# The mixtures' second product with tokens in the rows, its sums added from PSUM, and the second bias spread and added by GpSimd

## The reference, cut to what is computed

```python
x = L0_attn_a_x                                   # (2, 2048, 256), float32
x = x + _L0_attn_a_ref(_layernorm(x))             # 16 heads, causal
x = x + _L0_ffn_ref(_layernorm(x), Wr, W1, b1, W2, b2)
x = x + _L0_attn_b_ref(_layernorm(x), Wq, ...)    # distance attention
x = x + _L0_ffn_ref(_layernorm(x), Wr, W1, b1, W2, b2)

def _L0_ffn_ref(x, Wr, W1, b1, W2, b2):           # "mixture": 2 of 8 experts for each batch
    logits = x.mean(axis=1) @ Wr
    top_scores, top_idx = jax.lax.top_k(logits, 2)
    weights = jax.nn.softmax(top_scores, axis=-1)
    h = einsum('btd,bkdf->bktf', x, W1[top_idx]) + b1[top_idx][:, :, None, :]   # f = 1024
    h = gelu(h)
    y = einsum('bktf,bkfd->bktd', h, W2[top_idx]) + b2[top_idx][:, :, None, :]
    return einsum('bk,bktd->btd', weights, y)
```

## Time and profile before

| | |
|---|---|
| device time, median of three (lowest to highest) | 1783.35 us (1781.84 to 1784.34) |
| device time of the profiled execution | 1783.04 us |
| its span from first to last instruction | 1781.3 us |
| TensorE matmul busy | 1706.9 us, 96% |
| TensorE weight load busy | 1171.9 us, 66% |
| VectorE busy | 1062.4 us, 60% |
| ScalarE busy | 953.9 us, 54% |
| GpSimd busy | 352.7 us, 20% |
| mean granted TensorE clock | 0.993 |

### The profile page before, as it was taken

How to read it: one execution, slowest core, us unless ns; L and a number is a source line. 1 busy time by engine, 2 the same in 40 slices (tenths; PEclk the granted TensorE clock), 3 DMA queues, 4 the chain that set the end, 5 groups by cost and what they waited for, 6 DMA issues and landing times. The chain is left out here.

```text
span 1781.3 us, 28593 instructions
## 1 busy us (share of the span) xinstructions
PE 1706.9 (96%) x10767; PEld 1171.9 (66%) x10767; DVE 1062.4 (60%) x2216; ACT 953.9 (54%) x1258; POOL 352.7 (20%) x434
## 2 busy tenths in 40 slices
PE   5999999999998999999999999999999799999998
PEld 2222222222225888888878888889889688888886
DVE  6453433454325865775556687766896686577554
ACT  4999999999995322422225444554444332243221
POOL 3232223322210000000014344544334100000000
PEclk9999999999999999999999999999999899999999
DMA  3000000000020002000000000000000200300000
GB/s 119 1 1 1 1 1 1 2 1 1 2 95 1 1 7 89 1 1 1 1 0 1 1 1 1 1 2 1 1 1 25 71 1 1 119 12 13 13 13 24
DMA packets 24069, 28.10 MB, mean 16 GB/s; under 512 B 1319, under 2 KB 20862, under 8 KB 23934
## 3 DMA queue, kind: packets, MB, share of 16 engines
q1 hardware_dynamic: 23934, 26.27, 4.4%
HBM read 22.07 MB, written 4.19 MB: 15 GB/s over the span
## 5 line engine op out<-in xcount | busy, mean ns | idle before, releaser
L484 ACT ACTIVATE a_probs<-a_scores 128x1024 f32<-128x1024 f32 x544 | 503.9, 1131 | 35.5 <-PE a_scores L623 34.4
L1024 ACT ACTIVATE f_gelu<-f_h,f_bcol 128x512 f32<-128x512 f32 x256 | 176.6, 690 | 464.3 <-PE f_h L716 461.1
L599 PE MATMUL a_out<-a_probs,a_values 128*32 128x512 f32 (+3 forms) x2560 | 295.5, 543 | 9.4 <-ACT a_probs L484 7.7
L1084 DVE TENSOR_SCALAR f_hh<-f_gelu,f_gates 128x512 fp32r<-128x512 f32 x256 | 124.4, 486 | 242.8 <-ACT f_gelu L1024 241.6
L714 PE MATMUL f_h<-c_xhi,f_w1h 128*128 128x512 f32 x512 | 208.8, 408 | 13.3 <-DVE f_w1l L1058 13.3
L1501 ACT ACTIVATE d_score<-d_dist,d_nksq 128x512 f32<-128x512 f32 x128 | 92.8, 725 | 220.8 <-DVE d_dist L1641 220.8
L716 PE MATMUL f_h<-c_xhi,f_w1l 128*128 128x512 f32 x512 | 202.6, 396 | 0.0
L715 PE MATMUL f_h<-c_xlo,f_w1h 128*128 128x512 f32 x512 | 201.9, 394 | 0.0
L714 PE MATMUL f_ypsum<-f_hh,f_w2h 128*128 128x512 f32 x512 | 199.7, 390 | 0.0
L716 PE MATMUL f_ypsum<-f_hh,f_w2l 128*128 128x512 f32 x512 | 199.6, 390 | 0.0
L715 PE MATMUL f_ypsum<-f_hl,f_w2h 128*128 128x512 f32 x512 | 199.3, 389 | 0.0
(11 more groups left out here) (202 smaller groups left out, 2714.2 us busy)
## 6 DMA issues: line engine op xcount, KB each, us to landing
f_raw<-in_L_ffn_W SPq DMA_DIRECT2D x24, 512.0 KB, 7.8
x<-in_L_attn_a_x SPq DMA_DIRECT2D x8, 512.0 KB, 7.4
out<-x SPq DMA_DIRECT2D x8, 512.0 KB, 2.9
f_raw<-in_L_ffn_W SPq DMA_DIRECT2D x12, 256.0 KB, 3.3
early<-in_L_ffn_W SPq DMA_DIRECT2D x2, 256.0 KB, 3.0
distance_raw<-in_L_ffn_W SPq DMA_DIRECT2D x2, 256.0 KB, 3.6
distance_raw<-in_L_attn_b_Wv SPq DMA_DIRECT2D x1, 256.0 KB, 7.0
distance_raw<-in_L_attn_b_Wo SPq DMA_DIRECT2D x1, 256.0 KB, 6.6
```

The costliest lines, as they stand in the source:

```text
L484: act.activation(probs[:, u % UR], scores[:, 2 * (u % SR):2 * (u % SR) + 2, :], ACT.Exp, scale=HD ** -0.5)\
L599: mm = pe.matmul(spare[32 * j:32 * j + 32, i % 2, skip:skip + w], values[:, G % 2, kt + tile, j, :], probs[:, u % UR, j % 2, col:col + w], ...
L1024: act.activation(gel[:, n % HR, :], hps[:, n % 2, :], ACT.Gelu, bias=mix.bcol[:, q, FT * e + j:FT * e + j + 1])\
L1084: dve.tensor_scalar(hh[:, n % HR, :], gel[:, n % HR, :], gate, None, ALU.mult).then_inc(s_hh, 1)
```

## The change

The second product of a mixture step is laid out as `weighted` is: 128-token slices of `f_hh` and `f_hl` stand still and the 256 columns of W2 move. The result has tokens in the rows, two tiles in one bank, and is added to x straight from its banks. The turning of the result, `f_y`, `f_misc` and the copies with the bias go. The second bias now lies along the row: two rows b2 are fetched into `gathered`, weighted by their gates in their own partitions (`scale_b2`), summed and spread over all partitions by a product with ones (`widen_b2`), copied to `b2_wide` (`read_b2`), and added to each tile of x by GpSimd as soon as the tile has been normalised. VectorE's adds move from steps 5 and 6 of the next chunk to steps 3 and 4 and wait for GpSimd's. The column form of b2 and its two operations go.

```diff
@@ in head_attention, DVE at LAST + 3, and PE in last_group
                         mix.biases(dve, 0, spare[:, 0, :])
+                        mix.scale_b2(dve, 0)
+                        mix.read_b2(dve, 0, spare[:, 0, :])
...
+                    elif at == 34:
+                        spare_free()
+                        mix.widen_b2(pe, 0, spare[:, 0, :])
+                        routed.append((mix.s_b2w, 1))
@@ class Mixture
-        BR = self.BR = TOPK * (FT + KD)
+        BR = self.BR = TOPK * FT
...
-        self.b2w = sb(f"{st}_b2w", [P, NB, 2, KD], F32)
+        self.b2_rows = pr.gathered[0:TOPK, :]
+        self.own_gate = sb(f"{st}_own_gate", [TOPK, TOPK + 1], F32)
+        self.b2_wide = sb(f"{st}_b2_wide", [P, D], F32)
...
         for e, n in enumerate(chosen):
-            o = TOPK * FT + KD * e
             sp.dma_start(brow[FT * e:FT * e + FT, :], pr.b1[bass.ds(n, 1)].rearrange("o (j p) -> (o j) p", p=P)).then_inc(self.s_braw, 16)
-            sp.dma_start(brow[o:o + KD, :], pr.b2[bass.ds(n, 1)].rearrange("o (k p) -> (o k) p", p=P)).then_inc(self.s_braw, 16)
+        for e, n in enumerate(chosen):
+            sp.dma_start(self.b2_rows[e:e + 1, :], pr.b2[bass.ds(n, 1)]).then_inc(self.s_b2, 16)
...
+    def scale_b2(self, dve, q):
+
+        own = self.own_gate
         dve.wait_ge(self.s_gates, q + 1)
-        o = TOPK * FT
-        dve.tensor_scalar(b2w[:, q, 0, :], bcol[:, q, o:o + KD], gates[:, q, 0:1], None, ALU.mult).then_inc(self.s_b2w, 1)
...
+        dve.tensor_tensor(own[:, 0:TOPK], self.gate_cols[0:TOPK, q, :], self.pr.ident[0:TOPK, 0:TOPK], ALU.mult).then_inc(self.s_b2row, 1)
+        dve.wait_ge(self.s_b2row, 3 * q + 1)
+        dve.tensor_reduce(out=own[:, TOPK:TOPK + 1], in_=own[:, 0:TOPK], axis=AX.X, op=ALU.add).then_inc(self.s_b2row, 1)
+        dve.wait_ge(self.s_b2row, 3 * q + 2)
+        dve.wait_ge(self.s_b2, TOPK * 16 * (q + 1))
+        dve.tensor_scalar(self.b2_rows, self.b2_rows, own[:, TOPK:TOPK + 1], None, ALU.mult).then_inc(self.s_b2row, 1)
+
+    def widen_b2(self, pe, q, bank):
+        pe.wait_ge(self.s_b2row, 3 * q + 3)
+        pe.matmul(bank[:, 0:D], self.pr.ones[0:TOPK, :], self.b2_rows, start=True, stop=True).then_inc(self.s_b2turn, 1)
+
+    def read_b2(self, dve, q, bank):
+        dve.wait_ge(self.s_b2turn, q + 1)
+        if q >= 1:
+            dve.wait_ge(self.s_xb, TILES * q)
+        dve.tensor_copy(self.b2_wide[:], bank[:, 0:D]).then_inc(self.s_b2w, 1)
@@ def mixture: beside
-                          ("turn_biases", 47), ("biases", 48)) if at == when]
+                          ("turn_biases", 47), ("biases", 48), ("scale_b2", 48), ("widen_b2", 49), ("read_b2", 50)) if at == when]
@@ down, on TensorE
                     if e == 0 and j == 0 and chunk >= 2:
-                        pe.wait_ge(s_y, KD * (chunk - 1))
+                        pe.wait_ge(s_added, 2 * (chunk - 1))
                     pe.wait_ge(s_hl, n + 1)
-                    for k in range(KD):
-                        mm = split_product(pe, yps[:, KD * (chunk % 2) + k, :], w2h[:, e, j, k * P:(k + 1) * P],
-                                           w2l[:, e, j, k * P:(k + 1) * P], hh[:, n % HR, :], hl[:, n % HR, :],
-                                           e == 0 and j == 0, e == TOPK - 1 and j == FT - 1)
+                    for t in range(TPC):
+
+                        tokens = slice(t * P, (t + 1) * P)
+                        mm = split_product(pe, yps[:, KD * (chunk % 2) + t // 2, (t % 2) * D:(t % 2 + 1) * D], hh[:, n % HR, tokens],
+                                           hl[:, n % HR, tokens], w2h[:, e, j, :], w2l[:, e, j, :],
+                                           e == 0 and j == 0 and t % 2 == 0, e == TOPK - 1 and j == FT - 1, shared=True)
                     mm.then_inc(s_used, 1)
-
-                def turn_result(chunk, half):
...
@@ on VectorE: result goes, add_result reads the banks
-                def result(chunk):
...
+                def add_result(chunk, half):
                     dve.wait_ge(s_used, (chunk + 1) * CS)
...
+                    dve.wait_ge(mix.s_xb, chunk * TPC + 2 * half + 2)
                     xv = x[:, chunk * TPC + 2 * half:chunk * TPC + 2 * half + 2, :]
-                    dve.tensor_tensor(xv, xv, misc[:].rearrange("p (t d) -> p t d", t=2), ALU.add).then_inc(s_added, 1)
+                    dve.tensor_tensor(xv, xv, yps[:, KD * (chunk % 2) + half, :].rearrange("p (t d) -> p t d", t=2), ALU.add)\
+                       .then_inc(s_added, 1)
...
-                    if chunk >= 1 and at == 3:
-                        result(chunk - 1)
-                    if chunk >= 1 and at in (5, 6):
-                        add_result(chunk - 1, at - 5)
+                    if chunk >= 1 and at in (3, 4):
+                        add_result(chunk - 1, at - 3)
...
+            @block.gpsimd
+            def _(pool):
+
+                for tile in range(NB * TILES):
+                    pool.wait_ge(cols.s_xn, 2 * base + tile + 1)
+                    if tile % TILES == 0:
+                        pool.wait_ge(mix.s_b2w, tile // TILES + 1)
+                    pool.tensor_tensor(x[:, tile, :], x[:, tile, :], mix.b2_wide[:], ALU.add).then_inc(mix.s_xb, 1)
@@ in distance_attention
-              124: [("turn_biases",)]}
+              124: [("turn_biases",)],
+              125: [("scale_b2",)],
+              126: [("widen_b2",)]}
```

More of the change, by code:

```diff
@@ L859, in mixture @@
         routing = Routing(pr, st, 1, side)
[L860 to L862 removed]
+        s_wh, s_wl, s_h, s_gelu, s_hh, s_hl, s_used, s_added = (mix.s_wh, mix.s_wl, mix.s_h, mix.s_gelu, mix.s_hh, mix.s_hl,
+                                                                mix.s_used, mix.s_added)
         steps = [(q, c, e, j) for q in range(NB) for c in range(CHUNKS) for e in range(TOPK) for j in range(FT)]
@@ L946, in do @@
                         mix.turn_biases(pe, what, side)
+                    elif kind == "widen_b2":
+                        side_free(mix.s_b2w, what + 1)
+                        mix.widen_b2(pe, what, side)
                 def up(n):
@@ L967, in down @@
                     if e == 0 and j == 0 and chunk >= 2:
-                        pe.wait_ge(s_y, KD * (chunk - 1))
+                        pe.wait_ge(s_added, 2 * (chunk - 1))
                     pe.wait_ge(s_hl, n + 1)
-                    for k in range(KD):
-                        mm = split_product(pe, yps[:, KD * (chunk % 2) + k, :], w2h[:, e, j, k * P:(k + 1) * P],
-                                           w2l[:, e, j, k * P:(k + 1) * P], hh[:, n % HR, :], hl[:, n % HR, :],
-                                           e == 0 and j == 0, e == TOPK - 1 and j == FT - 1)
-                    mm.then_inc(s_used, 1)
-                def turn_result(chunk, half):
-                    n = chunk * (TPC // 2) + half
-                    pe.wait_ge(s_y, KD * (chunk + 1))
-                    if n >= 1:
-                        pe.wait_ge(s_added, n)
-                    for t in range(2):
-                        for k in range(KD):
-                            token = (2 * half + t) * P
-                            mm = pe.transpose(misc[:, (t * KD + k) * P:(t * KD + k + 1) * P], ysb[:, k, token:token + P], pr.ident[:])
-                    mm.then_inc(s_rturned, 1)
+                    for t in range(TPC):
[3 more added lines that the diff above has]
+                                           e == 0 and j == 0 and t % 2 == 0, e == TOPK - 1 and j == FT - 1, shared=True)
+                    mm.then_inc(s_used, 1)
                 for n in range(len(steps) + LAG):
@@ L991, in _ @@
                         down(n - LAG)
-                    chunk, at = divmod(n, CS)
-                    if 1 <= chunk < NB * CHUNKS and at in (4, 6):
-                        turn_result(chunk - 1, (at - 4) // 2)
                     if n < len(steps):
@@ L997, in _ @@
                             do(*work)
-                for half in range(2):
-                    turn_result(NB * CHUNKS - 1, half)
             @block.scalar
@@ L1053, in do @@
                         mix.biases(dve, what, side)
+                    elif kind == "scale_b2":
+                        mix.scale_b2(dve, what)
+                    elif kind == "read_b2":
+                        mix.read_b2(dve, what, side)
                     elif kind == "weights":
@@ L1058, in do @@
                         dve.tensor_tensor(lo, mix.raw(q, i), hi.bitcast(F32), ALU.subtract).then_inc(s_wl, 1)
-                def result(chunk):
-                    q = chunk // CHUNKS
+                def add_result(chunk, half):
                     dve.wait_ge(s_used, (chunk + 1) * CS)
-                    dve.wait_ge(mix.s_b2w, 2 * (q + 1))
-                    if chunk >= 1:
-                        dve.wait_ge(s_rturned, (TPC // 2) * chunk)
-                    for k in range(KD):
```

(20 more changed lines are left out.)

24 lines of the change are left out of this document (6 added, 18 removed).

## The result

The changed kernel takes 1790.67 us (median of five runs, 1789.01 to 1792.81), the kernel before 1782.70 us beside it (1781.39 to 1784.34). The ratio is 1.0045, 95% interval 1.0030 to 1.0059: slower by 8.0 us. The forecast was 1793.0 us in a range of 1785 to 1798, with a chance of 0.84 for slower; time and sign held. The profiled execution of after took 1792.81 us (span 1791.1) against 1783.04 us (span 1781.3) of before, so that pair differs by 9.8 us, where the sum said 10.0. It is the longest of its five runs, so the pair shows about 2 us more than the medians.

The account below looks back on a forecast made before the run. TensorE's starts-to-starts were taken to bound the mixtures. The terms +28.0 - 13.3 - 1.2 - 5.8 + 0.9 + 0.3 + 1.1 gave +10.0 us on the median of 1783.35, so 1793.0 us, range 1785 to 1798.

Parts of the forecast that it names:

- The new shape: Second product as twelve 256-column matmuls instead of six of 512: mixture step from 2.720 to 2.830 us, +28.0 us together.
- The turnings: Steady chunks of the mixtures lose 28 groups of four transposes of the result, 0.475 us each: -13.3 us.
- The side groups: The 30 groups that turn the normalised columns cost perhaps 0.04 us less each in the new mix: -1.2 us.
- The ends: At each mixture's end only two adds follow the last matmul, without copies and transposes: -2.9 us each, -5.8 us.
- The widening products: Four products of 256 columns spread the second bias, 0.3 us each, three on TensorE's path: +0.9 us.
- VectorE in the distance stage: The copy that reads the spread bias stands on VectorE ahead of the next distances: +0.3 us.
- GpSimd: Its 64 bias adds slow VectorE, unhidden at mixture starts and in the first chunk: +1.1 us, bounds 0 and 3.
- The clock: Distance stage starts at half clock after TensorE idles; the low stretch may vanish or last longer: +-1.4 us, centre 0.
- own pace: Rival: mixture matmuls of 512 columns keep 0.2267 us, 256-column ones take 0.12; +3.7 us, 1787 us; chance 0.16.
- A small gain: Rival: 256-column matmuls at 0.1175 us, 512-column ones at 0.2267, GpSimd free of cost; -5 us, 1778 us; chance 0.05.
- Short matmuls cost nothing extra: Rival: two 256-column matmuls take what one of 512 takes, mixture step stays 2.720 us; -16.8 us, 1766 us; chance 0.03.
- GpSimd starves VectorE: Rival: GpSimd's adds delay VectorE in the first chunks until TensorE waits; +6 us, 1799 us; chance 0.08.

Follow-up runs that it names:

- the rest alone put back in place: Changed kernel with the second product in its old 512-column shape and 32 unused bytes more in each mixture; 1765.50 us, ratio 0.9901 to the kernel before.
- the rest alone: Changed kernel with the second product back in six matmuls of 512 columns, as in the kernel before; 1778.63 us against 1781.99, ratio 0.9981.
- only the side bank moved: Changed kernel with the second product in its old shape and an unused PSUM bank ahead of the side bank; 1777.73 us, ratio 0.9970.
- the run of the new shape alone: Kernel before with only the second product written in the new shape; turning, copies, adds and column bias stay; 1804.76 us against 1781.99, ratio 1.0130.
- the run without the adds: Changed kernel without GpSimd's 64 adds of the second bias and VectorE's wait for them; 1789.93 us, ratio 1.0053.
- the kernel before with a hole: Kernel before with one unused block of 992 bytes per partition among the first mixture's small buffers; 1796.28 us against 1783.53, ratio 1.0076.
- the run with 64 bytes in each mixture: Kernel before with 64 unused bytes per partition in each mixture's small buffers, shifts of 64 and 128 bytes; 1792.94 us, ratio 1.0064.

## Why the prediction held, step by step

- **The new shape, +28.0 us.** Right in total, not in its reason. After shows 125 steps at 2.833 and 125 between 2.820 and 2.840. Taking the undisturbed ones, the first mixture pays 125 x 0.113 = 14.1 us and the second about 125 x 0.106 = 13.2, with the down-only steps some 27.8 us. But the shape itself costs 0.100 us at the places of before, 25 us; the other 2 to 3 us are the place of the operands, of which the prediction had nothing. The distance stage, from which 0.110 was read the earlier trace rows, is no clean price either: by the kernel's allocations its `d_phi` and `d_plo` start 128 bytes off the remainder by 256 of its other operands, and some of its steps last 2.825 us and others 2.835. That 0.110 came so near the 0.113 and 0.106 of after is in part luck.
- **The turnings, -13.3 us.** Confirmed, by one stretch of two profiled executions. From the first matmul of step 65 to that of step 128 of the first mixture, before takes 914.08 - 735.09 = 178.99 us, and the rest alone put back in place 908.89 - 733.71 = 175.18. Eight groups lie between: 0.476 us each, forecast 0.475.

```profile
735.09 0.39 PE L714 MATMUL f_h<-c_xhi,f_w1h 128*128 128x512 f32 x1
...
914.08 0.39 PE L714 MATMUL f_h<-c_xhi,f_w1h 128*128 128x512 f32 x1
```
```profile
733.71 0.39 PE L720 MATMUL f_h<-c_xhi,f_w1h 128*128 128x512 f32 x1
...
908.89 0.39 PE L720 MATMUL f_h<-c_xhi,f_w1h 128*128 128x512 f32 x1
```

- **The side groups, -1.2 us.** The two steps around one last 3.187 + 2.913 us, 0.434 over two undisturbed ones; forecast 0.44. Against 0.476 this is -1.3 us for 30.
- **The ends, -5.8 us.** Measured -2.78 and -3.15, -5.9 us; the last add ends 1.60 us after the last matmul starts, where 1.8 was expected.
- **The widening products, +0.9 us.** The term that was mis-sized. The earlier trace rows hold two instructions in 0.63 us, and I read them as two products. They are one: a product of this kernel in plain float32 shows as two instructions (its float32 transposes show as one, x128 for 128 of them in the earlier trace rows). The same in after:

```profile
697.70 0.69 PE L847 MATMUL f_side<-gathered,ones 2*128 2x256 f32 x2
698.32 0.50 PE L720 MATMUL f_h<-c_xhi,f_w1h 128*128 128x512 f32 x1
```

  Four calls give eight instructions in the groups of after. The two steps around this one last 3.547 + 2.933 us, 0.81 over 5.667. The one in the second mixture costs the same (3.536 + 2.930 us). If the one in the distance stage does too, the three make +2.4 us, 1.5 more than forecast. I should have compared the count of the row with the number of calls in the code.
- **VectorE in the distance stage, +0.3, and GpSimd, +1.1 us.** Neither can be seen in a time. The reading copy in the distance stage (0.42 us at 1392.77) is done 1.02 us before the next distances can start, which wait for TensorE. The row scaling takes 0.34 us in the first mixture and 1.47 in the distance stage, where GpSimd works beside it (timeline of DVE), and TensorE doesn't wait for it:

```profile
695.89 0.34 DVE L843 TENSOR_SCALAR gathered<-gathered,f_own_gate 2x256 f32<-2x256 f32 x1
...
1389.72 1.47 DVE L843 TENSOR_SCALAR gathered<-gathered,f_own_gate 2x256 f32<-2x256 f32 x1
```

  TensorE's first wait in the first mixture is 3.67 us as in the earlier trace rows, where +0.35 was expected, and the way from the first to the 17th step grows by 1.5 and 1.4 us, just what 13 dearer steps cost (13 x 0.100 to 0.113). The distance stage as a whole differs by over 1 us between runs of one and the same code (471.35 in the rest alone, 469.97 with only the side bank moved), so of its +1.2 us no more than the widening product is put down to the change.
- **The clock, +-1.4 us.** At the start of the distance stage the second to the sixth matmul now follow each other at 0.23 us and the next ones at 0.43 (timeline of PE), where in the earlier trace rows the stretch at 1.2 GHz came at once. The granted clock from 931 to 934 us is 0.79 on the mean, since this stretch holds some of both levels, 2.4 and 1.2 GHz. The slow stretch moved and did not vanish.

```profile
931.32 0.47 PE L720 MATMUL d_outs<-c_xhi,wq_hi 128*128 128x512 f32 x1 [3.01 <-PEq L106]
...
932.33 0.40 PE L721 MATMUL d_outs<-c_xlo,wq_hi 128*128 128x512 f32 x1
932.56 0.47 PE L722 MATMUL d_outs<-c_xhi,wq_lo 128*128 128x512 f32 x1
932.83 0.63 PE L720 MATMUL d_outs<-c_xhi,wq_hi 128*128 128x512 f32 x1
```
```profile
931.00:934.00 3.00, 2.68 (x9) 2.21 (x10) 2.68 (x4) 0.93 (x2) 2.70 (x4) 0.79 0.00 0
```

With the measured terms the sum is 27.8 - 13.3 - 1.3 - 5.9 + 2.4 = +9.7 us against 9.8 in the profiled pair. The sum on record came to +10.0 because the GpSimd and VectorE terms, 1.4 us too high, stood against the widening products, 1.5 us too low: that these two errors cancel is luck. Against the medians' +8.0 us the forecast is 2 us too high.

The rivals: "own pace" falls with the run of the new shape alone (2.820 where it wants 2.800, and 512s at 0.231 instead of 0.2267 us). "A small gain" falls with the same steps. "Short matmuls cost nothing extra" falls with the same run. "GpSimd starves VectorE" falls with the run without the adds. The fact that nearly upset the case was in none of them: that moving buffers by 992 bytes slows matmuls whose shape nobody touched. It did little harm here only because the new shape hardly feels it (2.833 against 2.820 us, where the old shape has 2.787 against 2.720).

## What to carry to other kernels

A change that adds or drops a small buffer also moves every later one: compare the start-to-start time of untouched matmuls before crediting a gain or loss to the edit, and try a pad. Take prices from starts, with the exact mix of shapes, and check the count of a row against the calls in the code before dividing by it. When the parts of a change don't add up to the whole, look for something that all of them share; here it was the places in SBUF.

## What was unexpected of the hardware

- **The pace of float32r matmuls depends on where their operands lie in SBUF.** The step of twelve matmuls of 512 columns takes, by the shift of the weights / of hh and hl against the kernel before: 0/0: 2.720 us; 1024/1024 and 2048/2048: 2.720; 32 bytes (hh and hl alone): 2.787; 64/64: 2.780; 128/128: 2.766; 992/992: 2.787; 1984/1984: 2.773; 32 for the weights and 256 for hh and hl: 2.800. In the kernel before the second mixture's operands lie 4864 bytes (19 x 256) above the first's and both run at 2.720. All this fits a remainder by 256 bytes (128 more is slow, and 4864 is no multiple of 512), in which every operand of before, the normalized columns included, has the same value. Whether that value itself counts or only that it is the same for all was not tried in a mixture, and why matmuls whose own operands stayed slow down too is open.
- **Moving all operands together changes nothing, as far as the distance stage shows.** The buffers of its steps lie behind the small buffers of both mixtures, so the runs move all of them at once: by 992 bytes in the kernel before with a hole, 128 in the run with 64 bytes in each mixture, 1984 in after. In all of these, and in before, seven undisturbed steps last 19.80 to 19.82 us. With the hole of 992 bytes, to hold against the earlier trace rows:

```profile
1232.16 0.40 PE L714 MATMUL d_banks<-d_qhi,d_khi 128*128 128x512 f32 x1
...
1251.97 0.40 PE L714 MATMUL d_banks<-d_qhi,d_khi 128*128 128x512 f32 x1
```

  So what counts seems to be the places of the operands to each other. This mix of 512s and 256s feels places little, though (next point but one), so for the twelve 512s it stays open.
- The Trainium skill, "SBUF — State Buffer", section "Operand start alignment", asks of an operand's start only that it is a multiple of the element size, and says that this is about legality and not speed. Every place here keeps that rule; the runs add that the speed differs by up to 3% between such places.
- **The new shape is less sensitive.** With 256 columns in down the same shifts cost 0.013 us a step in the first mixture and 0 to 0.020 in the second, against 0.067 and 0.053 for the old one.
- **Float32 products show as two instructions**, 0.62 us to the next start for 256 columns, and with the matmuls behind them 0.81 us in all.
